# Low rank of a pair's two tiles turned together by one transpose

## Chip, cores and metric

The kernel runs on one core of one Trainium2 chip. The time is the device time of one execution in microseconds (us); the median of several runs counts.

## The reference

Two layers are computed on x, 32 samples of 64 rows by 1024 columns (2048 rows in all). The change touches the first one only. Its low rank part, cut to what matters:

```python
out = conv1d(x, weight, groups=4) + ctx + bias            # h, 2048 rows x 1024
y = h @ W.T + b                                           # 1024 x 1024
scores = h @ gate_w.T + gate_b                            # 4 ranks: 8, 16, 32, 64
pick the rank r with the highest softmax score (top 1; its weight is normalised to 1)
y = y + (h @ A[:r].T) @ B[:, :r].T                        # A: 64 x 1024, B: 1024 x 64
x = x + y
```

The second layer has the same form, with a mixture over 8 kernels in place of the convolution and a router over 8 experts of rank 16 in place of the ranks.

## The kernel before

**Tiles and pairs.** 128 rows are a tile, two tiles are a pair: tiles T = 0 to 15 and pairs g = 0 to 7 are the first layer, tiles 16 to 31 and pairs 8 to 15 the second. s = T % 2 says which tile of its pair a tile is. Pairs 0 and 1 are done plainly; from pair 2 (`FULL`) on the dense product of a pair is done in seven block products P1 to P7 in the manner of Strassen and Winograd. The code of each engine is one list written out by hand, with semaphores between the engines; the order in the code is the order on the engine.

**Two parts for each number.** The matmuls run in fp32r, and each float is split in a high part (ScalarE's cast, `a_hi`, `s_hi`, `ut_hi`) and the rest (VectorE's subtraction, `a_lo`, `s_lo`), so a product has three matmuls: high by high, high by low, low by high.

**A tile's low rank.** The plain matmuls (`plain`, L1265 and L1266, into `b_p`) also give the 64 low rank columns and the 4 scores of a tile. VectorE works out the gate (`gate0`, a chain of small instructions) and writes the gated low rank into `u_sb[:, s, :]`, 128 rows by 128, the 64 columns twice (L932). TensorE turns it by a transpose (`turn_u`, L1303) into `b_u`, so that the 64 ranks lie on partitions 0 to 63 and once more on 64 to 127. ScalarE casts all 128 partitions to `ut_hi` (L585) and the first 64 to `ut_lo` (L587); VectorE then overwrites partitions 64 to 127 of `ut_hi` with the rest (L890). `lb_hi` holds B twice, one above the other, so the one matmul `ut_hi` by `lb_hi` (L1311) gives high by high and low by high, and the second, `ut_lo` by `lb_lo` (L1313), the high by low part and the bias.

**A pair's order on TensorE** (g = 2 to 7): plain of both tiles, P1 into `b_x`, first half of the next pair's first convolution into `b_m` (L1231), **transpose of tile 2g**, P2 into `b_z`, second half of that convolution into `b_y`, **transpose of tile 2g + 1**, P4 into `b_w`, P5 into `b_y`, low rank of tile 2g into `b_z` and `b_p` (its first weight load waits for `utlo_done`, which L890 signals), a convolution, P6, a convolution into `b_z`, low rank of tile 2g + 1, P7, P3 and what is left.

**VectorE and ScalarE in that stretch.** VectorE: gates, `sum_mix` of the convolution's halves (L867), the `ut_hi` split of tile 2g between them, `a_lo` of the next pair's blocks A11 and A12 (L875, each after ScalarE's `a_hi`, L566), the `ut_hi` split of tile 2g + 1, and in pairs 3 to 6 four `prep_lo` splits (L824). In those four pairs GpSimd also forms sums of the second layer's weights (`praw`, L499 to L504) as soon as their load has landed; ScalarE casts them (L612).

## Time and profile before

| | |
|---|---|
| median of 3 runs | 506.79 us (505.94 to 506.85) |
| the profiled execution | 505.61 us |
| its span, first to last instruction | 503.9 us |
| TensorE's granted clock, mean | 1.000 of full |
| busy: TensorE, VectorE, ScalarE, GpSimd | 99%, 69%, 26%, 28% |
| first layer's pairs 2 to 7 | about 83 to 266 us of the span |

The busy shares count instructions in flight. Matmuls overlap, so a matmul's own duration is longer than what it adds to TensorE's list; the distance from one start, or from one piece of the chain, to the next is what it costs there.

### The profile page before, as it was taken

How to read it: one execution, taken by the hardware profiler on the slowest of the kernel's cores; microseconds unless marked ns; L12 is line 12 of the kernel's file. 1: busy time of each engine (PE TensorE's matmuls, PEld its weight loads, DVE VectorE, ACT ScalarE, POOL GpSimd, SP SyncE). 2: the span in 40 equal slices, each digit the busy share in tenths (PEclk: the TensorE clock that was granted, in tenths of full speed). 3: DMA queues.
4: the chain of work that ended last, by engine and by line, in shares of the span. 5: the costliest groups of instructions: out<-in, count | busy, mean ns of one | idle time of the engine just before them, and what ended most of it. 6: DMA issues, size and time to landing. Idle time of an engine off the chain costs nothing.

```text
span 503.9 us, 8309 instructions
## 1 busy us (share of the span) xinstructions
PE 499.1 (99%) x2981; PEld 467.7 (93%) x2981; DVE 347.9 (69%) x824; ACT 130.4 (26%) x272; POOL 142.0 (28%) x122
## 2 busy tenths in 40 slices
PE   8999999999999999999999999999999999999997
PEld 8999999999999999999999899999999999999986
DVE  3966988857766685776897975665747566574753
ACT  4732334212233122331252321210212111111200
POOL 1000010003443142431205462441516244152620
PEclk9999999999999999999999999999999999999999
DMA  8845204428476574657899752433425233340212
GB/s 317 320 144 166 91 1 148 157 89 262 163 245 195 196 231 171 197 184 268 273 410 339 298 168 87 145 102 126 130 69 161 85 129 103 134 138 19 103 47 84
DMA packets 41125, 84.34 MB, mean 167 GB/s; under 512 B 3803, under 2 KB 24667, under 8 KB 41084
## 3 DMA queue, kind: packets, MB, share of 16 engines
q1 hardware_dynamic: 31884, 61.16, 36.6%
q10 hardware_dynamic: 9200, 22.65, 12.3%
q8 instruction: 24, 0.39, 0.3%
q14 instruction: 17, 0.14, 0.1%
HBM read 58.82 MB, written 24.97 MB: 166 GB/s over the span
## 4 chain that ended last, share of the span: by engine, by line
PE 98%; DMA 1%; DVE 1%; issue 0%; ACT 0%; DVEq 0%
PE b_p L1265 10%; PE b_x L1283 7%; PE b_x L1286 7%; PE b_x L1285 7%; PE b_m L1231 6%; PE b_p L1266 5%; PE b_y L1285 5%; PE b_y L1286 5%; PE b_y L1283 5%; PE b_m L1241 3%; PE b_w L1283 2%; PE b_z L1285 2%; PE b_w L1285 2%; PE b_z L1286 2%; PE b_z L1283 2%; PE b_w L1286 2%
## 5 line engine op out<-in xcount | busy, mean ns | idle before, releaser
L566 ACT CAST a_hi<-mixed 128x512 fp32r<-128x512 f32 x63 | 38.1, 620 | 167.4 <-DVE mixed L870 88.3
L1265 PE MATMUL b_p<-wp,a_hi 128*128 128x464 f32 (+1 forms) x224 | 72.5, 377 | 0.0
L512 POOL TENSOR_TENSOR xs<-xs,mixw_sb 128x464 f32<-128x464 f32 (+1 forms) x28 | 36.3, 1307 | 115.2 <-DMA xs<-x_scratch 81.5
L1266 PE MATMUL b_p<-wp,a_lo 128*128 128x232 f32 (+1 forms) x224 | 60.0, 268 | 0.0
L882 DVE TENSOR_TENSOR s_lo<-mixed,s_hi 128x512 fp32r<-128x512 f32 x56 | 45.4, 834 | 20.5 <-ACT s_hi L578 20.5
L578 ACT CAST s_hi<-mixed 128x512 fp32r<-128x512 f32 x56 | 34.7, 621 | 77.3 <-POOL mixed L484 41.2
L875 DVE TENSOR_TENSOR a_lo<-mixed,a_hi 128x512 fp32r<-128x512 f32 x63 | 47.4, 779 | 9.4 <-ACT a_hi L566 8.8
L484 POOL TENSOR_TENSOR mixed<-mixed 128x512 f32<-128x512 f32 x13 | 17.6, 1353 | 120.9 <-DVE a_lo L875 120.9
L976 DVE TENSOR_TENSOR xs<-b_x,xs 128x464 f32<-128x464 f32 (+1 forms) x54 | 33.5, 620 | 22.9 <-PE b_x L1286 20.0
L1265 PEld LDWEIGHTS b_p<-wp,a_hi 128*128 128x128 f32 x224 | 42.0, 188 | 4.7
L1266 PEld LDWEIGHTS b_p<-wp,a_lo 128*128 128x128 f32 x224 | 42.7, 191 | 0.2
L1283 PE MATMUL b_y<-wb_hi,s_hi 128*128 128x464 f32 (+1 forms) x112 | 41.2, 368 | 0.0
L1285 PE MATMUL b_y<-wb_lo,s_hi 128*128 128x464 f32 (+1 forms) x112 | 41.1, 367 | 0.0
L1286 PE MATMUL b_y<-wb_hi,s_lo 128*128 128x464 f32 (+1 forms) x112 | 41.1, 367 | 0.0
L1231 PE MATMUL b_m<-first_in,blk 128*128 128x128 f32 x256 | 32.0, 278 | 0.2 <-DMA blk<-in_xblk 0.2
L976 DVE TENSOR_TENSOR xs<-b_y,xs 128x432 f32<-128x432 f32 (+1 forms) x28 | 17.4, 620 | 20.8 <-PE b_y L1286 20.0
L1231 PEld LDWEIGHTS b_m<-first_in,blk 128*128 128x128 f32 x256 | 30.8, 194 | 0.7 <-DMA blk<-in_xblk 0.5
L1283 PE MATMUL b_x<-wb_hi,s_hi 128*128 128x432 f32 (+1 forms) x80 | 30.5, 381 | 0.0
L1286 PE MATMUL b_x<-wb_hi,s_lo 128*128 128x432 f32 (+1 forms) x80 | 29.2, 365 | 0.0
L1285 PE MATMUL b_x<-wb_lo,s_hi 128*128 128x432 f32 (+1 forms) x80 | 29.2, 365 | 0.0
L1283 PEld LDWEIGHTS b_y<-wb_hi,s_hi 128*128 128x128 f32 x112 | 21.0, 188 | 2.0
L1286 PEld LDWEIGHTS b_y<-wb_hi,s_lo 128*128 128x128 f32 x112 | 21.0, 188 | 1.9
(260 smaller groups left out, 1210.0 us busy)
## 6 DMA issues: line engine op xcount, KB each, us to landing
blk<-x_scratch SPq DMA_DIRECT2D x16, 512.0 KB, 3.3
blk<-in_xblk SPq DMA_DIRECT2D x14, 516.0 KB, 3.9
xs<-in_x SPq DMA_DIRECT2D x16, 296.0 KB, 3.6
x_scratch<-xs SPq DMA_DIRECT2D x16, 296.0 KB, 4.5
w_raw<-in_wcat SPq DMA_DIRECT2D x8, 546.0 KB, 8.3
xs<-x_scratch SPq DMA_DIRECT2D x14, 280.0 KB, 3.2
out_dram<-xs SPq DMA_DIRECT2D x14, 280.0 KB, 2.5
praw<-in_wcat ACTq DMA_DIRECT2D x8, 464.0 KB, 6.1
```

What stands on the lines that cost most here:

```text
L512: pool.tensor_tensor(x_rows, x_rows, bbase[:, a:b], ALU.add).then_inc(x_biased[q], 1)
L566: act.copy(a_hi[:, op, :, :], mixed[:, op, :, :]).then_inc(ahi_done[op], 1)
L578: act.copy(s_hi[:, i, :, :], mixed[:, S_AT[i], :, :]).then_inc(shi_done[i], 1)
L875: dve.tensor_tensor(a_lo[:, op, :, :], mixed[:, op, :, :], hi(a_hi[:, op, :, :]), ALU.subtract).then_inc(alo_done[op], 1)
L882: dve.tensor_tensor(s_lo[:, i, :, :], mixed[:, S_AT[i], :, :], hi(s_hi[:, i, :, :]), ALU.subtract).then_inc(slo_done[i], 1)
L976: dve.tensor_tensor(x_rows, src[:, 0:HALF[l]], x_rows, ALU.add).then_inc(done, 1)
L1231: ins = pe.matmul(dst, blk[s][:, at + side:at + side + QB], taps, start=(side == 0), stop=(side == 1))
L1265: pe.matmul(both, x_hi, wp[:, k, :, 0:PLAIN[l]], start=(k == 0), stop=False, skip_group_check=True)
L1266: ins = pe.matmul(dst, x_lo, wp_hi[:, k, 0:PLAIN[l]], start=False, stop=(k == NCH - 1), skip_group_check=True)
L1283: pe.matmul(dst, x_hi[:, k, :], w_hi[:, k, :], start=(first and k == 0), stop=False, skip_group_check=not first)
L1285: pe.matmul(dst, x_hi[:, k, :], w_lo[:, k, :], start=False, stop=False, skip_group_check=not first)
L1286: ins = pe.matmul(dst, x_lo[:, k, :], w_hi[:, k, :], start=False, stop=(k == HK - 1), skip_group_check=not first)
```

## The change

In pairs 2 to 7 (`together`), the gate of tile 2g writes its 64 columns once into columns 0 to 63 of `u_sb[:, 0, :]`, that of tile 2g + 1 into columns 64 to 127. One transpose (`turn_pair`), at the place of the second, turns both: tile 2g lies on partitions 0 to 63 of `b_u`, tile 2g + 1 on 64 to 127. Each tile's high part is cast to its own half of `ut_hi[:, s, :]` and to `ut_lo[0:64]`, and VectorE writes the rest to the other half. The transpose of tile 2g goes, and its casts and its split move behind `split_a(A12, g + 1)` on both engines. Pairs 0, 1 and the second layer stay.

```diff
+        def together(T):
+            return 2 * FULL <= T < TILES
+        def turned_rows(s):
+            return slice(RANK * s, RANK * (s + 1))
...
@@ ScalarE, split_ut
+                if together(T):
+                    rows_ = turned_rows(s)
+                    act.copy(ut_hi[rows_, s, :], b_u[rows_, 0:P]).then_inc(uthi_done, 1)
+                    act.copy(ut_lo[0:RANK, s, :], b_u[rows_, 0:P]).then_inc(uthi_second, 1)
+                    return
...
@@ ScalarE, a pair
-                split_ut(2 * g)
+                if not together(2 * g):
+                    split_ut(2 * g)
                 if g < LAST:
                     split_a(A11, g + 1)
...
                 if g < LAST:
                     split_a(A12, g + 1)
+                if together(2 * g):
+                    split_ut(2 * g)
                 split_ut(2 * g + 1)
...
@@ VectorE, split_ut
+                if together(T):
+                    rows_ = turned_rows(s)
+                    dve.wait_ge(uthi_second, T + 1)
+                    dve.tensor_tensor(ut_hi[turned_rows(1 - s), s, :], b_u[rows_, 0:P], hi(ut_hi[rows_, s, :]),
+                                      ALU.subtract).then_inc(utlo_done, 1)
...
@@ VectorE, gate0
+                if together(T):
+                    dve.wait_ge(ut_done, T - s)
...
+                    if together(T):
+                        dve.tensor_scalar(u_sb[:, 0, RANK * s + r0:RANK * s + r], hid[:, r0:r],
+                                          kw[:, j:j + 1], None, ALU.mult).then_inc(gated, 1)
...
@@ VectorE, a pair
                 if g == FULL:
-                    split_ut(2 * g)
...
                 if g < LAST:
                     split_a(A11, g + 1)
                     split_a(A12, g + 1)
+                if together(2 * g):
+                    split_ut(2 * g)
                 split_ut(2 * g + 1)
...
@@ TensorE
+            def turn_pair(g):
+                pe.wait_ge(gated, 4 * (2 * g + 2))
+                pe.wait_ge(utlo_done, 2 * g)
+                pe.wait_ge(uthi_second, 2 * g)
+                pe.transpose(b_u[:, 0:P], u_sb[:, 0, :], ident[:, :]).then_inc(ut_done, 2)
...
-                turn_u(t1)
+                if not together(t1):
+                    turn_u(t1)
...
                     mixture(t1 + 2, 1, b_y)
-                    turn_u(t2)
+                    if together(t1):
+                        turn_pair(g)
+                    else:
+                        turn_u(t2)
```

On VectorE in pair 3, before the change, from the end of the second gate to the `prep_lo` splits (names are those above; `praw` are the weights in preparation):

```order
L932 TENSOR_SCALAR u_sb<-hid_sb,kw 128x2x32
L976 TENSOR_TENSOR xs<-b_x,xs 128x432 [waits x_loaded0,p1_done]
L867 TENSOR_TENSOR mixed<-b_m,ctx_row 128x8x64 [waits ctx_loaded,mix_done,slo_done3,slo_done1]
L890 TENSOR_TENSOR ut_hi<-b_u,ut_hi 64x128 [waits uthi_done]
L867 TENSOR_TENSOR mixed<-b_y,ctx_row 128x8x64 [waits ctx_loaded,mix_done,slo_done3,slo_done1]
L875 TENSOR_TENSOR a_lo<-mixed,a_hi 128x512 [waits ahi_done0]
L875 TENSOR_TENSOR a_lo<-mixed,a_hi 128x512 [waits ahi_done1]
L890 TENSOR_TENSOR ut_hi<-b_u,ut_hi 64x128 [waits uthi_done]
L824 TENSOR_TENSOR prep_lo<-praw,prep_hi 128x464 [waits prep_sum,phi_done] x4
```

The same stretch after the change (the line numbers are the changed kernel's):

```order
L956 TENSOR_SCALAR u_sb<-hid_sb,kw 128x32
L1003 TENSOR_TENSOR xs<-b_x,xs 128x432 [waits x_loaded0,p1_done]
L883 TENSOR_TENSOR mixed<-b_m,ctx_row 128x8x64 [waits ctx_loaded,mix_done,slo_done3,slo_done1]
L883 TENSOR_TENSOR mixed<-b_y,ctx_row 128x8x64 [waits ctx_loaded,mix_done,slo_done3,slo_done1]
L891 TENSOR_TENSOR a_lo<-mixed,a_hi 128x512 [waits ahi_done0]
L891 TENSOR_TENSOR a_lo<-mixed,a_hi 128x512 [waits ahi_done1]
L908 TENSOR_TENSOR ut_hi<-b_u,ut_hi 64x128 [waits uthi_second,uthi_done] x2
L840 TENSOR_TENSOR prep_lo<-praw,prep_hi 128x464 [waits prep_sum,phi_done] x4
```

The split of tile 6 stood ahead of the second `sum_mix`; now both splits stand behind both `a_lo`.

On TensorE in pair 3, before, around the transpose of tile 6 (the product after it is P2):

```order
L1231 MATMUL b_m<-first_in,blk 128x8x16 [waits blk_loaded0,sum_done,agg_read]
L1231 MATMUL b_m<-first_in,blk 128x8x16 x7
L1303 MATMUL b_u<-ident,u_sb 128x128 [waits uthi_second,utlo_done,gated]
L1283 MATMUL b_z<-wb_hi,a_hi 128x432 [waits sum_done]
L1285 MATMUL b_z<-wb_lo,a_hi 128x432
```

And after:

```order
L1257 MATMUL b_m<-first_in,blk 128x8x16 [waits blk_loaded0,sum_done,agg_read]
L1257 MATMUL b_m<-first_in,blk 128x8x16 x7
L1309 MATMUL b_z<-wb_hi,a_hi 128x432 [waits sum_done]
L1311 MATMUL b_z<-wb_lo,a_hi 128x432
```

The convolution is now followed by P2 directly; nothing else moves on TensorE up to the second transpose, which stays where it was.

## Rows read from the trace of the kernel before

**Rows 1.** The page: TensorE's busy time and share; then the chain that ended last.

```profile
PE 499.1 (99%) x2981; PEld 467.7 (93%) x2981; DVE 347.9 (69%) x824; ACT 130.4 (26%) x272; POOL 142.0 (28%) x122
...
PE 98%; DMA 1%; DVE 1%; issue 0%; ACT 0%; DVEq 0%
```

**Rows 2.** Times of TensorE's transposes, all 32 (ns, minimum, median, maximum).

```profile
L1303 PE MATMUL b_u<-ident,u_sb x32: 270/272/328, 33.8 to 487.1; 128*128 128x128 f32 x32
```

**Rows 3.** Chain of work, pair 4, around tile 8's transpose: start, duration, what.

```profile
154.81 0.56 PE b_m L1231 x5
155.37 0.11 PE b_u L1303
155.48 0.20 PE b_z L1283
```

**Rows 4.** Chain of work, pair 4, convolution straight ahead of a product.

```profile
166.27 0.56 PE b_m L1231 x5
166.83 0.20 PE b_x L1283
```

**Rows 5.** Order of time, pair 3, VectorE: start, duration, instruction, [idle before, releaser].

```profile
128.74 0.69 DVE L867 TENSOR_TENSOR mixed<-b_y,ctx_row 128x512 f32<-128x512 f32 x1 [2.25 <-PE b_y L1231]
130.11 3.13 DVE L875 TENSOR_TENSOR a_lo<-mixed,a_hi 128x512 fp32r<-128x512 f32 x2 [0.69 <-ACT a_hi L566]
133.28 0.29 DVE L890 TENSOR_TENSOR ut_hi<-b_u,ut_hi 64x128 fp32r<-64x128 f32 x1
```

**Rows 6.** Pair 3, VectorE, narrower stretch: the second a_lo by itself.

```profile
131.60 1.65 DVE L875 TENSOR_TENSOR a_lo<-mixed,a_hi 128x512 fp32r<-128x512 f32 x1
```

**Rows 7.** Pair 3, TensorE's weight loads at tile 6's first low rank matmul.

```profile
133.06 0.19 PEld L1311 LDWEIGHTS b_z<-lb,ut_hi 128*128 128x128 f32 x1
```

**Rows 8.** Pair 3, TensorE's matmuls at the same place.

```profile
133.45 0.36 PE L1313 MATMUL b_z<-lb,ut_lo 97*128 97x432 f32 x1
```

**Rows 9.** Pair 3, GpSimd.

```profile
127.47 1.19 POOL L499 TENSOR_TENSOR praw<-praw 128x464 f32<-128x464 f32 x1 [8.96 <-DMA praw<-in_wcat]
...
129.90 1.20 POOL L502 TENSOR_TENSOR praw<-praw 128x464 f32<-128x464 f32 x1
131.18 1.53 POOL L504 TENSOR_TENSOR praw<-praw 128x464 f32<-128x464 f32 x1
```

**Rows 10.** Tile 1's low rank, VectorE: end of the split that TensorE waited for.

```profile
47.13 0.29 DVE L890 TENSOR_TENSOR ut_hi<-b_u,ut_hi 64x128 fp32r<-64x128 f32 x1
```

**Rows 11.** Tile 1's low rank, weight loads.

```profile
47.48 0.19 PEld L1311 LDWEIGHTS b_z<-lb,ut_hi 128*128 128x128 f32 x1 [0.30 <-DVE ut_hi L890]
```

**Rows 12.** Tile 1's low rank, matmuls.

```profile
47.78 0.36 PE L1313 MATMUL b_z<-lb,ut_lo 97*128 97x432 f32 x1
```

**Rows 13.** VectorE, pairs 2, 4 and 7: the odd tile's ut_hi split.

```profile
100.09 0.29 DVE L890 TENSOR_TENSOR ut_hi<-b_u,ut_hi 64x128 fp32r<-64x128 f32 x1
...
163.33 0.29 DVE L890 TENSOR_TENSOR ut_hi<-b_u,ut_hi 64x128 fp32r<-64x128 f32 x1
...
253.20 0.29 DVE L890 TENSOR_TENSOR ut_hi<-b_u,ut_hi 64x128 fp32r<-64x128 f32 x1
```

**Rows 14.** Weight loads, the same pairs: the even tile's first low rank matmul.

```profile
101.16 0.19 PEld L1311 LDWEIGHTS b_z<-lb,ut_hi 128*128 128x128 f32 x1
...
164.07 0.19 PEld L1311 LDWEIGHTS b_z<-lb,ut_hi 128*128 128x128 f32 x1
...
255.30 0.19 PEld L1311 LDWEIGHTS b_z<-lb,ut_hi 128*128 128x128 f32 x1
```

**Rows 15.** Pair 3, VectorE, later: the last use of b_z.

```profile
136.46 0.60 DVE L976 TENSOR_TENSOR xs<-b_z,xs 128x432 f32<-128x432 f32 x1
```

**Rows 16.** Pair 3, weight loads: the convolution that overwrites b_z.

```profile
137.84 0.19 PEld L1231 LDWEIGHTS b_z<-first_in,blk 128*128 128x128 f32 x1
```

**Rows 17.** Pair 4, VectorE, ahead of that split.

```profile
161.12 1.20 DVE L875 TENSOR_TENSOR a_lo<-mixed,a_hi 128x512 fp32r<-128x512 f32 x1 [0.69 <-ACT a_hi L566]
162.61 0.69 DVE L875 TENSOR_TENSOR a_lo<-mixed,a_hi 128x512 fp32r<-128x512 f32 x1 [0.29 <-ACT a_hi L566]
```

More of the change, by code:

```diff
@@ L888, in split_ut @@
                 dve.wait_ge(uthi_done, T + 1)
-                if T < TILES:
+                if together(T):
[3 more added lines that the diff above has]
+                                      ALU.subtract).then_inc(utlo_done, 1)
+                elif T < TILES:
                     dve.tensor_tensor(ut_hi[RANK:P, s, :], src[RANK:P, :], hi(ut_hi[RANK:P, s, :]),
@@ L918, in gate0 @@
                 hid = hidden(T)
-                if T > 1:
+                if together(T):
+                    dve.wait_ge(ut_done, T - s)
+                elif T > 1:
                     dve.wait_ge(ut_done, T - 1)
@@ L931, in gate0 @@
                 for j, r in enumerate(RANKS):
-                    dve.tensor_scalar(u_sb[:, s, :].rearrange("p (d r) -> p d r", d=2)[:, :, r0:r],
-                                      hid[:, r0:r].unsqueeze(1).to_broadcast([P, 2, r - r0]),
-                                      kw[:, j:j + 1], None, ALU.mult).then_inc(gated, 1)
+                    if together(T):
+                        dve.tensor_scalar(u_sb[:, 0, RANK * s + r0:RANK * s + r], hid[:, r0:r],
+                                          kw[:, j:j + 1], None, ALU.mult).then_inc(gated, 1)
+                    else:
+                        dve.tensor_scalar(u_sb[:, s, :].rearrange("p (d r) -> p d r", d=2)[:, :, r0:r],
+                                          hid[:, r0:r].unsqueeze(1).to_broadcast([P, 2, r - r0]),
+                                          kw[:, j:j + 1], None, ALU.mult).then_inc(gated, 1)
                     r0 = r
@@ L1147, in _ @@
                     take_first(g)
-                if g == PAIRS - 1:
-                    split_ut(2 * g)
                 if g < LAST:
                     sum_mix(2 * g + 2, 0)
-                if g not in (FULL, PAIRS - 1):
+                if not together(2 * g):
                     split_ut(2 * g)
@@ L1515, in _ @@
                     mixture(t1 + 2, 1, b_y)
-                    turn_u(t2)
+                    if together(t1):
+                        turn_pair(g)
+                    else:
+                        turn_u(t2)
                 if g == FULL:
```

## The prediction, made before the changed kernel ran

> **What bounds the kernel now.** I read the page first. TensorE is busy 99% of the span and 98% of the chain that ended last is TensorE [rows 1]. So the end moves only by what TensorE's list gets shorter and by what TensorE newly waits for. Then the chain of work in order of time, around one of the transposes: it shows what each piece adds to the list, which a matmul's own duration does not. Then, in order of time, the stretch of each pair where the moved work has to be ready. The question for the reader is: how late does VectorE finish the split that tile 2g's low rank waits for, once that split stands behind both `a_lo`?
>
> **The removed transposes.** One goes in each of pairs 2 to 7, so six. A transpose lasts 0.27 us by its own duration [rows 2], but in the chain it is a piece of 0.11 us between the last of the convolution and P2 [rows 3]. Where a convolution is followed by a product with no transpose between, the next piece begins at once and the product's first piece is as long as there, 0.20 us [rows 3, 4]. So taking the transpose out leaves no gap of its own behind. 6 x 0.11 = 0.66 us less. The transpose overlaps its neighbours, and I take the 0.11.
>
> The Trainium skill (TensorE: Matmul & The Clock Gate, Part 4: PE-mode transpose) gives about 275 ns for a 128 by 128 transpose in a kernel's context. The duration here agrees (0.27 us), the piece of the chain does not. Six at that price would be 1.65 us, as in the second rival below.
>
> **Work on the other engines.** The four multiplications that end a gate write 64 columns rather than 128, the casts cover 64 partitions rather than 128 at the same free size, and the number of casts and splits is unchanged. The nearest row for the split, which now crosses to the other half of the partitions, is the one of before with the same 128 columns, 0.29 us [rows 5]. None of it is on TensorE's list; I cost it at nothing, covered by TensorE's products, except where it is late. What it costs without that cover is the next step.
>
> **The moved split, pair by pair.** Tile 2g's split now takes the place of tile 2g + 1's: directly behind the second `a_lo`. It then has to be done before the weight load of tile 2g's first low rank matmul, where the old one had been done long ago.
>
> Pair 2: the split at that place begins at 100.09 and ends at 100.38, the weight load begins at 101.16 [rows 13, 14]: 0.78 us to spare. Pair 4: 163.33 + 0.29 = 163.62 against 164.07, 0.45 us to spare; pairs 5 and 6 repeat pair 4 to within 0.01 us. Pair 7: 253.49 against 255.30, 1.8 us [rows 13, 14]. A signal takes about 0.06 us: tile 1's split ended at 47.13 + 0.29 = 47.42 and the load that waited for it began at 47.48 [rows 10, 11]. So these five pairs pass without a wait. That TensorE comes there 0.11 us earlier doesn't change it: the convolution half that starts the `sum_mix`, `a_hi`, `a_lo` chain also comes 0.11 us earlier.
>
> Pair 3 doesn't pass. There the two `a_lo` take 3.13 us together [rows 5], the second 1.65 us [rows 6], where the same instruction takes 0.69 us in pair 4 [rows 17]. In the same microseconds GpSimd works on `praw`, up to 131.18 + 1.53 = 132.71, and the second `a_lo` ends 0.54 us after that, at 133.25 [rows 6, 9]. In pair 4 the first `a_lo` is lengthened too, to 1.20 us, but it is over before the second is ready [rows 17]. GpSimd began so late in pair 3 because it waited for the load of `praw` [rows 9], 8.96 us. So the split there begins at 133.28 and ends at 133.57 [rows 5], and the weight load begins at 133.06 [rows 7]. After the change this load waits: it would begin at 133.57 + 0.06 = 133.63. A load that has waited has its second matmul 0.30 us later (47.48 to 47.78) [rows 11, 12], here at 133.93; before it was at 133.45 [rows 8], and with the transpose gone it would be at 133.34. The wait costs 133.93 - 133.34 = 0.59 us if GpSimd's end holds VectorE where it is, and 0.48 us if VectorE, too, comes 0.11 us earlier. I take 0.59, since what ends last ahead of the split is GpSimd, started by a load and not by TensorE.
>
> **What is queued behind.** Both splits behind each other put the four `prep_lo`, the taking of P5 and the first takings from `b_z` about 0.3 us later (one more split of 0.29 us). The closest user is the convolution that overwrites `b_z`: its last taking ends at 136.46 + 0.60 = 137.06, the weight load begins at 137.84 [rows 15, 16], 0.78 us to spare, more than 0.3. ScalarE's order only puts two casts behind two others; the `prep` casts have no user as near. Nothing more is added.
>
> **The sum.** -0.66 + 0.59 = -0.07 us, against the profiled execution's 505.61 us, which lies 1.18 us below the median of the runs shown. On the median: 506.79 - 0.07 = 506.7 us. This is no difference that can be measured: what can be told from no change here is about 0.2%, 1.0 us.
>
> **Rivals.**
>
> *No wait at all.* The wait in pair 3 hangs on when a load lands. If GpSimd's sums ended 0.6 us sooner or so, the second `a_lo` would end sooner by as much and the wait would be gone; landing later by about as much lets the first `a_lo` go ahead of a GpSimd sum and also shortens it. For it: GpSimd's start is set by a transfer [rows 9], which nothing ties to TensorE. Against: nothing in the change moves that load. Time: -0.66 us, 506.1 us; still within 0.2%.
>
> *The full duration comes back.* If each transpose gave back its 0.27 us [rows 2], six would give 1.63 us, and without a wait the time were 505.2 us, faster by 0.3%. Against: the chain's piece of 0.11 us [rows 3]. With the wait in pair 3 it were 505.8 us, at the edge.
>
> *Slower: the wait in all four preparing pairs.* If in pairs 4 to 6 as well the second `a_lo` is held by GpSimd. The point from which it decides: 0.45 - 0.06 = 0.39 us of lateness in a pair is free. With pair 3's 0.59 us in all four the sum is -0.66 + 2.36 = +1.7 us, 508.5 us; with three of the four it is +1.1 us, just slower. For it: the first `a_lo` of pair 4 is already lengthened to 1.20 us [rows 17]. Against: in those pairs it ends at 162.32, 0.29 us before the second is ready at 162.61 [rows 17], so GpSimd must be more than 0.6 us later for a first effect.
>
> The Trainium skill (SBUF — State Buffer, Who interferes with whom) says that a VectorE instruction with two inputs in SBUF and a GpSimd instruction that reads SBUF block each other whole, whichever came first holding. The second `a_lo` ending 0.54 us after GpSimd agrees. By that rule the split itself, with one input in PSUM, is not held, and only the order of the two engines at the moment decides pair 3.
>
> **How the numbers follow.** My forecast (a wait in pair 3 alone, 0.3 to 0.85 us): 0.56. No wait: 0.22. Full duration back: 0.09. Slower: 0.08. The remaining 0.05 is for what I don't see, half to each side. The predicted time is 506.7 us. Faster 0.11 (full duration, 0.02 of the rest), same 0.79, slower 0.10. The likeliest case with the runs' own spread of half a us to each side reaches from 506.0 to 507.3; the case without a wait pulls the low end to 505.5 (506.1 less that spread), and the high end stays at 507.3. Both far rivals lie outside.
>
> **What would show it.** In the chain of the changed kernel no `b_u` piece between the convolution into `b_m` and P2 in pairs 2 to 7, and P2 0.11 us closer to the convolution's end. Among the waits one of the weight load of `b_z<-lb,ut_hi` for VectorE's `ut_hi` split in pair 3, 0.5 to 0.6 us, none in pairs 2, 4, 5, 6 and 7. The first matmul of pair 8's plain part some 0.1 us earlier than now, with 0.2 to 0.7 us gained between single pairs. I am wrong if P2 comes by 0.2 us or more closer, if a `ut_hi` split lasts longer than 0.35 us, if weight loads wait in pairs 4 to 6, or if a wait arises at the overwriting of `b_z`.

## The result: 0.47% slower, where no difference was forecast

The changed kernel takes 508.52 us (median of 22 runs, 505.98 to 511.64), the kernel before 506.26 us (22 runs, 505.06 to 508.54) on the same chips. The ratio is 1.0047, interval [1.0033, 1.006]: slower by more than the 0.2% that a measurement here can tell, and above the range of 505.5 to 507.3. The profiled execution of the changed kernel took 507.78 us, its span is 506.0 us, 2.1 more than that of before, both at a granted clock of 1.0. In 8 of the 22 executions of the changed kernel TensorE's mean granted clock was 0.996 or 0.997 (beside the experiments, in 5 of 156 executions of the kernel before); the other 14 have a median of 508.2 us, so the clock is the smaller part of the loss (see e9).

The page of the changed kernel, the lines that answer to [rows 1]:

```profile
PE 499.3 (99%) x2975; PEld 467.3 (92%) x2975; DVE 346.5 (68%) x824; ACT 131.4 (26%) x272; POOL 141.8 (28%) x122
...
PE 84%; DMA 7%; DVE 3%; POOL 2%; issue 1%; ACT 1%; ACTq 0%; SPq 0%; DVEq 0%; POOLq 0%
```

TensorE has six matmuls fewer, and yet the end is no longer set by TensorE alone: 7% of the chain is DMA. The waits of TensorE in the changed kernel (engine, line, releaser: us in total, times, longest) name the two places:

```profile
PEld b_x L1309 <- DVE xs L1003: 1.8, 1, 1.8
PE b_x L1309 <- DVE xs L1003: 1.7, 1, 1.7
...
PEld b_z L1344 <- DVE ut_hi L908: 0.7, 1, 0.7
```

The last line is the forecast wait in pair 3. The first two are P7 of pair 7 (its weight load and its first matmul), and nothing in the prediction speaks of it.

**The removed transposes.** The chain of work of the changed kernel in pair 4, against [rows 3]:

```profile
154.15 1.78 PE b_m L1257 x16
155.94 0.20 PE b_z L1309
```

The convolution ends at 155.93, and P2 follows at once. Matching TensorE's matmuls of both traces one by one, the changed kernel's lead grows by 0.09 to 0.11 us at each of the six places, as the pieces of 0.11 us said. Ahead of pair 2, where the two kernels do the same, the changed one is already 0.18 us behind in this execution.

**Pair 3.** VectorE, the weight load and the matmuls of the changed kernel, against [rows 5, 7, 8], and GpSimd against [rows 9]:

```profile
130.12 3.25 DVE L891 TENSOR_TENSOR a_lo<-mixed,a_hi 128x512 fp32r<-128x512 f32 x2 [0.69 <-ACT a_hi L574]
133.39 0.61 DVE L908 TENSOR_TENSOR ut_hi<-b_u,ut_hi 64x128 fp32r<-64x128 f32 x2
```

```profile
133.73 0.19 PEld L1344 LDWEIGHTS b_z<-lb,ut_hi 128*128 128x128 f32 x1 [0.67 <-DVE ut_hi L908]
```

```profile
133.73 0.47 PE L1344 MATMUL b_z<-lb,ut_hi 128*128 128x432 f32 x1 [0.31 <-DVE ut_hi L908]
134.04 0.36 PE L1346 MATMUL b_z<-lb,ut_lo 97*128 97x432 f32 x1
```

```profile
131.29 1.52 POOL L512 TENSOR_TENSOR praw<-praw 128x464 f32<-128x464 f32 x1
```

GpSimd ends at 132.81, the second `a_lo` 0.56 us later at 133.37, the split for tile 6 at 133.69, and the load begins at 133.73. The second matmul is at 134.04 and was at 133.45. Before the wait the two traces were 0.01 us apart at this point, behind it 0.59: the wait costs 0.60 us, where the sum had 0.59.

**Pair 7.** The rest of the loss is here. The chain of work of the changed kernel at P7:

```profile
252.19 7.76 DMA xs<-in_x
...
259.97 0.34 DVE xs L1016
...
261.17 0.40 DVE wb_lo L844
...
262.20 0.61 DVE xs L1003
262.81 0.04 issue
262.86 0.47 PE b_x L1309
```

P7 writes `b_x` and has to wait until VectorE has taken P6 out of it. VectorE comes to that late, since two takings ahead of it waited for the rows of pair 7 to land, as VectorE's own rows say. First before, where the same two wait for nothing, then the changed kernel:

```profile
255.85 0.61 DVE L976 TENSOR_TENSOR xs<-b_y,xs 128x432 f32<-128x432 f32 x1
...
256.89 0.32 DVE L989 TENSOR_TENSOR xs<-b_p,xs 128x160 f32<-128x160 f32 x1
```

```profile
257.81 0.61 DVE L1003 TENSOR_TENSOR xs<-b_y,xs 128x432 f32<-128x432 f32 x1 [0.87 <-DMA xs<-in_x]
...
259.97 0.33 DVE L1016 TENSOR_TENSOR xs<-b_p,xs 128x160 f32<-128x160 f32 x1 [1.04 <-DMA xs<-in_x]
```

P7 comes at 262.86, before at 260.85:

```profile
260.85 0.39 PE L1283 MATMUL b_x<-wb_hi,s_hi 128*128 128x432 f32 x1
```

The shift against before grows there from +0.17 to +2.01 us, and to +2.2 us further on.

**Back to the root.** SP's queue on either side of that, first before, then the changed kernel:

```profile
237.37 0.32 SPq L342 DMA_DIRECT2D x_scratch<-xs  x1
242.91 0.33 SPq L337 DMA_DIRECT2D xs<-in_x  x1
243.34 0.85 SPq L342 DMA_DIRECT2D x_scratch<-xs  x2
247.91 0.83 SPq L337 DMA_DIRECT2D xs<-in_x  x2
```

```profile
238.31 0.32 SPq L350 DMA_DIRECT2D x_scratch<-xs  x1
244.07 0.33 SPq L345 DMA_DIRECT2D xs<-in_x  x1
244.50 0.85 SPq L350 DMA_DIRECT2D x_scratch<-xs  x2
251.81 0.81 SPq L345 DMA_DIRECT2D xs<-in_x  x2
```

A pair's rows are stored and loaded in quarters (0 and 1 are the halves of the first tile's rows, 2 and 3 of the second's). The first line is the store of quarter 2 of pair 6. SP then waits until it has landed and loads that quarter for pair 7 (`stored(2, g)`, `load_x(2, g + 1)`). Only behind that stand the stores of quarters 3 and 1, and behind their landing the loads of these two. The store of quarter 2 is 0.94 us later. The two others are 1.16 us later, and their landing, which the next loads wait for, takes 7.3 us where it took 4.6 (243.34 to 247.91, 244.50 to 251.81). Only the second of the two lands later: 6.8 us after its own issue, before 4.1 us; the first takes 3.1 us and took 3.2. What runs beside them is a load of 928 KB on ScalarE's queue, in the changed kernel at:

```profile
244.56 0.65 ACTq L743 DMA_DIRECT2D wp_place<-in_wcat  x1
```

Before, it was issued 0.95 us behind the first of the two stores (244.29), now 0.06 us behind it.

The lateness of quarter 2's store comes from the split that was moved, by way of a transfer. VectorE in pair 6, before and then the changed kernel:

```profile
225.34 0.29 DVE L890 TENSOR_TENSOR ut_hi<-b_u,ut_hi 64x128 fp32r<-64x128 f32 x1
225.67 2.30 DVE L824 TENSOR_TENSOR prep_lo<-praw,prep_hi 128x464 fp32r<-128x464 f32 x4
```

```profile
225.97 0.66 DVE L908 TENSOR_TENSOR ut_hi<-b_u,ut_hi 64x128 fp32r<-64x128 f32 x2
226.67 1.75 DVE L840 TENSOR_TENSOR prep_lo<-praw,prep_hi 128x464 fp32r<-128x464 f32 x3
```

`prep_lo` begins 1.00 us later: 0.27 because TensorE is behind by that much (0.18 from the start of the trace, and what pair 3's wait leaves beyond the transposes gone by then), 0.37 for the second split, and 0.36 more because the second `sum_mix` of the pair comes late (see the open points). ScalarE stores `prep_lo`, waits for the landing, loads it home, and only then makes `a_hi`. ScalarE before and in the changed kernel:

```profile
234.88 1.14 ACT L566 CAST a_hi<-mixed 128x512 fp32r<-128x512 f32 x2 [9.02 <-DMA ts_lo_scratch<-prep_lo]
```

```profile
235.82 1.15 ACT L574 CAST a_hi<-mixed 128x512 fp32r<-128x512 f32 x2 [8.61 <-DMA ts_lo_scratch<-prep_lo]
```

The lateness passes through the wait for this transfer nearly whole, 0.94 us. VectorE's `a_lo` follows, and behind it on VectorE's list the taking that releases quarter 2's store.

A second part is the landing of that store: 5.5 us before, 5.7 in the changed kernel, and 5.4 to 6.6 us over all profiled executions. Counted from the start of pair 7, e1 and e13 issue it only 0.10 us later than before, it lands after 6.6 and 6.5 us, and the two stores behind it come at +5.5 and +5.4. So in some executions most of their lateness comes from this landing and not from the split. What makes it longer wasn't tried.

### The profile page after: what moved, and what is told of

It reads as the page before. It is cut to its first block, busy times and chain, and to the rows that moved or that the text cites. A ratio compares the mean times of both kernels' runs of the same rounds, so it can differ in the third digit from the quotient of the medians.

```text
span 506.0 us, 8309 instructions
## 1 busy us (share of the span) xinstructions
PE 499.3 (99%) x2975; PEld 467.3 (92%) x2975; DVE 346.5 (68%) x824; ACT 131.4 (26%) x272; POOL 141.8 (28%) x122
## 4 chain that ended last, share of the span: by engine, by line
PE 84%; DMA 7%; DVE 3%; POOL 2%; issue 1%; ACT 1%; ACTq 0%; SPq 0%; DVEq 0%; POOLq 0%
PE b_p L1291 8%; PE b_x L1309 6%; PE b_x L1312 6%; PE b_x L1311 6%; PE b_m L1257 4%; PE b_p L1292 4%; PE b_y L1311 4%; PE b_y L1309 4%; PE b_y L1312 4%; PE b_m L1267 3%; DMA x_scratch<-xs 2%; PE b_z L1311 2%; PE b_w L1309 2%; PE b_w L1311 2%; PE b_z L1309 2%; PE b_z L1312 2%
```

## The experiments

In the table every time is counted from the start of pair 7 (its first matmul `b_p<-wp,a_hi`, in the changed kernel at 239.27), in each kernel's profiled execution: when the stores of quarters 3 and 1 were issued, when the loads behind them were, how long lies between, when VectorE took `b_p` (which needs the second of these loads), and what P7's first matmul waited. The executions differ by chance already ahead of pair 2, by up to 0.8 us, so spans of single executions are not compared without that. The load of `wp_place` was issued at +5.29 to +5.34, but at +6.75 and +6.33 in e7 and e12.

| kernel | median us | ratio to before | stores | loads | between | `b_p` taken | P7 waits |
|---|---|---|---|---|---|---|---|
| before | 506.26 | | +4.35 | +8.92 | 4.6 | +17.89 | 0 |
| changed | 508.52 | 1.0047 | +5.22 | +12.54 | 7.3 | +20.70 | 1.7 |
| e9, changed again | 509.14 | 1.0060 | +5.75 | +13.72 | 8.0 | +22.30 | 2.9 |
| e1, not pair 3 | 507.07 | 1.0014 | +5.53 | +12.15 | 6.6 | +20.38 | 1.3 |
| e3, splits early | 505.48 | 0.9984 | +5.06 | +9.81 | 4.8 | +18.07 | 0 |
| e5, not pair 6 | 504.82 | 0.9971 | +4.38 | +9.15 | 4.8 | +18.24 | 0 |
| e7, load later | 505.69 | 0.9987 | +5.88 | +10.52 | 4.6 | +19.77 | 1.3 |
| e8, before + lateness | 509.11 | 1.0032 | +5.82 | +12.85 | 7.0 | +19.87 | 0.3 |
| e12, e3 + e7 | 505.20 | 0.9979 | +4.97 | +9.49 | 4.5 | +18.06 | 0 |
| e13, pair 6 alone | 506.24 | 0.9997 | +5.40 | +12.16 | 6.8 | +19.41 | 0.2 |
| e14, pair 3 alone | 506.32 | 0.9995 | +5.10 | +12.43 | 7.3 | +19.35 | 0.1 |
| e15, not pair 7 | 505.94 | 0.9986 | +5.69 | +12.67 | 7.0 | +19.36 | 0 |
| e16, pair 7 alone | 505.80 | 0.9990 | +4.41 | +8.96 | 4.6 | +18.25 | 0 |
| e17, stores first | 505.20 | 0.9983 | +2.25 | +6.91 | 4.7 | +18.53 | 0 |
| e18, before, stores first | 506.05 | 1.0001 | +2.42 | +6.84 | 4.4 | +18.54 | 0 |

Four more runs (e2, e6, e10, e11) have a fault in their edits, and e4 touches none of this; they are not in the table. In a pair that is taken back, tile 2g's split stood in its general place on VectorE's list, behind the first `sum_mix`. But in the kernel before, pairs 2 and 7 have it further ahead: ahead of the splits of S, and ahead of that `sum_mix`. So in e2, e6 and e10 (pair 7), and in e10 and e11 (pair 2), the second tile's transpose came 0.5 to 1.3 us later for waiting for a split, which neither kernel does in the trace. They are told, but settle nothing about a pair; e13 to e16 are the same questions without that fault.

**e1: all but pair 3.**

```
 def together(T):
-    return 2 * FULL <= T < TILES
+    return 2 * FULL <= T < TILES and T // 2 != 3
```

> The change, but pair 3 is left as before. Two places theory (the wait for VectorE's split in pair 3 costs 0.6 us by itself; some 1.8 us more arise in pair 7, where the rows of pair 7 are loaded late): about 0.5 us less than the changed kernel if the late loads stay, so 1.7 to 2.0 us above the kernel before; in the trace no wait of the weight load of b_z in pair 3, and a wait of the first matmul of P7 in pair 7. Rival, one place theory (the late split in pair 3 pushes everything behind it, the late loads too): all of the loss goes, at or 0.6 us under the kernel before.

507.07 us, ratio 1.0014 [0.9985, 1.0043]. The wait in pair 3 is gone from the trace, that of P7 in pair 7 is still there (1.3 us). Three of its twelve executions had a granted clock of 0.996 or 0.997, and they are the three slowest (509.4 to 510.8 us). So pair 3 is a part of the loss at most, and pair 7's wait doesn't need it.

**e2: all but pairs 6 and 7.**

```
-    return 2 * FULL <= T < TILES
+    return 2 * FULL <= T < 12
```

> The change in pairs 2 to 5 only, pairs 6 and 7 as before. Two places theory: the loss in pair 7 goes, the wait in pair 3 stays: 4 x 0.11 = 0.44 us saved, 0.6 us lost, within 0.3 us of the kernel before; the loads of pair 7's rows are issued near 248 us, not 252 us. Rival (the lateness that reaches pair 7 comes from pair 3 on): still 1.5 us or more above the kernel before.

506.18 us, 0.9999 [0.9973, 1.0025]. P7 doesn't wait, but the second transpose of pair 7 does, 1.3 us, by the fault named above.

**e3: both splits early,** on ScalarE and VectorE ahead of the next pair's `a_hi` and `a_lo`.

```
-                if not together(2 * g):
-                    split_ut(2 * g)
+                split_ut(2 * g)
+                if together(2 * g):
+                    split_ut(2 * g + 1)
                 if g < LAST:
                     split_a(A11, g + 1)
...
-                if together(2 * g):
-                    split_ut(2 * g)
-                split_ut(2 * g + 1)
+                if not together(2 * g):
+                    split_ut(2 * g + 1)
```

> The change, with both ut splits of a pair moved ahead of a_hi and a_lo of block A11, on ScalarE and on VectorE, directly behind the second sum_mix, where VectorE idles 0.69 us until ScalarE has cast. If late splits are the only cause of both losses (two places theory with its root in the order of VectorE), no weight load waits in pair 3, prep_lo and all behind it comes at the time of before or earlier, the loads of pair 7 are issued near 248 us, and the time is 0.66 us under the kernel before (0.4 to 1.0). Rival (lateness has another root, such as the one transpose itself or chance in the transfers): about as slow as the changed kernel, 1.5 us or more above before.

505.48 us, 0.9984 [0.9961, 1.0007]; span 503.1, 0.8 less than before. There is no wait in pair 3 and none in pair 7, and TensorE ends 0.73 us ahead of before. Some 0.33 of that stood already ahead of pair 2, by chance; each removed transpose but the last then gave 0.09 to 0.10 us, the last 0.05, and 0.1 us is lost again behind them.

**e4: what a transpose costs in TensorE's list.** The kernel before with four more transposes beside each of 12, 48 in all, written where nobody reads.

```
+                if 2 * FULL <= T < TILES:
+                    for _ in range(4):
+                        pe.transpose(b_u[:, 2 * P:3 * P], u_sb[:, s, :], ident[:, :])
                 pe.transpose(b_u[:, P * s:P * s + P], u_sb[:, s, :], ident[:, :]).then_inc(ut_done, 1)
```

> The kernel before with four more transposes of the same u_sb in front of each of the twelve transposes of tiles 4 to 15, into unused columns of b_u: 48 more, output unchanged. If a transpose costs the 0.11 us of its piece in the chain: 5.3 us slower (up to 6 with knock-on in transfers). If it costs its 0.27 us: 13 us slower.

510.91 us, 1.0089 [1.0059, 1.012], 4.8 us over the median of before on that chip. The chain of work of e4 in pair 4:

```profile
155.30 1.78 PE b_m L1231 x16
157.08 0.43 PE b_u L1305 x4
157.52 0.11 PE b_u L1306
157.63 0.20 PE b_z L1283
```

Four more are 0.43 us, and TensorE is 5.1 us later at the end: 0.11 us each. The price of 0.27 us, 13 us for 48, is refuted.

**e5: all but pair 6.**

```
-    return 2 * FULL <= T < TILES
+    return 2 * FULL <= T < TILES and T // 2 != 6
```

> The change in all pairs but pair 6, which is as before. If the loss in pair 7 has its root in pair 6, where the four prep_lo come one split later, it goes: 5 x 0.11 = 0.55 us saved, 0.6 us lost in pair 3, so within 0.3 us of the kernel before. If its root is the moved order within pair 7, or chance: 1.2 us or more above before.

504.82 us, 0.9971 [0.9954, 0.9988], the lowest median of the study. Against the changed kernel one pair has been taken back, and 3.7 us of the median have gone. The gain over before is more than its five transposes explain (0.55 us, 0.11%), though the interval reaches to 0.12%.

**e6: all but pair 7,** as e5 with `T < 14`.

> The change in all pairs but pair 7. If the root of the loss is pair 6: the rows of pair 7 are loaded late here too, and the loss stays, 1 to 2 us above before. If it is pair 7's own moved order: 5 x 0.11 = 0.55 us saved, 0.6 us lost in pair 3, within 0.3 us of before.

507.61 us, 1.0023 [1.0003, 1.0042], with the fault; the wait of 1.2 us is at the second transpose of pair 7. See e15.

**e7: the load of `wp_place` later.** In the changed kernel four small copies stand ahead of its issue on ScalarE.

```
                     act.wait_ge(pl_done, 2 * PAIRS)
+                    for i in range(4):
+                        act.copy(spare[:, P * i:P * (i + 1)], ones[:, :]).then_inc(first_hi, 1)
+                    act.wait_ge(first_hi, 5)
```

> The change, with four small copies on ScalarE, which idles there, in front of the 928 KB load of the second layer's plain weights in pair 7, so that the load is issued some 0.8 us later. If the two stores of pair 6's rows, issued 0.07 us ahead of it in the changed kernel and 0.94 us ahead before, are late because they share the transfer engines with this load: stores have landed within 5 us instead of 7.3, the first matmul of P7 in pair 7 waits less than 0.5 us instead of 1.7, and the time is 1 to 1.8 us under the changed kernel, 0.3 to 1 us above before. If the collision is not the cause: as slow as the changed kernel.

505.69 us, 0.9987 [0.9972, 1.0003]: 2.8 us under the median of the changed kernel, with the change itself whole. The stores, 0.87 us ahead of the load now, land after 4.6 us. In the profiled execution (507.31 us, over the median) P7 waits 1.3 us nonetheless, but not for the rows: no taking waits for them. VectorE waits for ScalarE's casts of the held back load and of the next one, and the takings stand behind:

```profile
255.72 2.16 DVE L854 TENSOR_TENSOR wp<-wp_place,wp 128x928 fp32r<-128x928 f32 x2 [1.73 <-ACT wp L671]
260.70 1.12 DVE L848 TENSOR_TENSOR wb_lo<-wb_raw,wb_hi 128x928 fp32r<-128x928 f32 x1 [0.47 <-ACT wb_hi L666]
```

So this cure has a price of its own, and its median shows the sum of both.

**e8: the lateness alone.** The kernel before, with four small subtractions on VectorE in pair 6 ahead of `prep_lo`.

```
+                if g == PREP_LAST:
+                    for i in range(4):
+                        dve.tensor_tensor(spare[:, P * i:P * (i + 1)], ident[:, :], ones[:, :], ALU.subtract)
                 if PREP_FIRST <= g <= PREP_LAST:
                     for b in (0, 1, 3, 2):
```

> The kernel before, with four small subtractions (128 by 128, into unused memory, 0.6 to 1 us in all) on VectorE in pair 6 alone, between the odd tile's ut split and the prep_lo; no transpose is touched. If lateness of VectorE in pair 6 is what starts the loss in pair 7: pair 6's stores are issued within 0.3 us of the load of the plain weights, the rows of pair 7 are loaded late, and the kernel is 1 to 2 us slower than before. If VectorE's lateness there is harmless: no change, within 0.3 us of before.

509.11 us (505.95 to 510.64), 1.0032 [1.0009, 1.0056]. Nothing of the change is in this kernel, and its median is as high as that of the changed one. Its executions fall in two groups: five at 506.0 to 507.5 us, as before, and seven at 508.8 to 510.6, of which five had a granted clock of 0.995 to 0.997. So the lateness makes the loss in a part of the executions. The profiled one (507.46 us) is of the lower group: the stores are at +5.82, 7.0 us lie between, the second transpose of pair 7 waits 0.3 us and P7 another 0.3. It was 0.77 us behind before already ahead of pair 2, and loses 0.9 us in pair 7.

**e9: the changed kernel again,** on another chip.

> The changed kernel once more, for a second profiled execution. Two things are asked of it. The wait in pair 3 should come only if GpSimd starts its sums about 12.7 to 12.8 us after the pair's first plain matmul (before and the first trace of the changed kernel); from 13.0 us on the two a_lo take about 0.8 us each and nothing waits. The late rows in pair 7 should come again, with the wait of P7 or of the transpose's successor: time 1.7 to 3 us above before.

509.14 us, 1.006 [1.0038, 1.0081]. Both waits are there again, 0.7 us for the weight load in pair 3 and 2.9 us at P7. Here the wait has a sequel. In stretches of the profile (busy us and instructions of each engine, then PEclk, TensorE's granted clock as a share of full speed) during the wait, behind it, and later:

```profile
261.30:264.20 2.90, 0.00 (x0) 0.00 (x0) 2.82 (x6) 0.62 (x1) 0.00 (x0) 1.00 1.02 419
264.90:268.10 3.20, 3.20 (x10) 2.92 (x10) 3.01 (x6) 0.62 (x1) 0.00 (x0) 0.50 1.01 421
269.00:275.00 6.00, 6.00 (x36) 5.63 (x36) 4.17 (x7) 1.24 (x2) 4.38 (x3) 1.00 0.95 299
```

TensorE did nothing for 2.9 us; its granted clock then fell from 1.00 to 0.50, 1.2 GHz in place of 2.4, for at least the 3.2 us shown. P7's matmuls start 0.36 us apart there and 0.20 at full clock, which puts TensorE 1.6 us further back. In the changed kernel's profiled execution, with 1.7 us of waiting, the clock stays at 1.00. The executions at 0.993 to 0.997 (8 of 22 of the changed kernel, 5 of 12 of e8, 4 of 9 of e9) fit such a fall, but only this one was profiled.

**e10 and e11: pair 3 alone, pair 7 alone** (`together` true for that pair).

> The change in pair 3 alone. If its wait were there in every execution, 0.59 - 0.11 = 0.5 us slower than before; as five of seven profiled executions with pair 3 in the new order or near it had no wait there, I expect -0.1 to +0.5 us, a median within 0.3 us of before. If pair 3's lateness by one split reaches pair 7's loads through the transfers, more than 1 us slower.

> The change in pair 7 alone. In the kernel before, the transpose of tile 15 follows tile 14's split on VectorE by less than 0.1 us in the profiled execution, so any lateness of VectorE there stops TensorE (as in the trace of the kernel that left pairs 6 and 7). With pair 7 changed that link is gone. If this link costs the kernel before something in most executions, the median falls by 0.5 us or more, more than the 0.11 us of one transpose; if not, it falls by 0.1 us, which can't be told from nothing.

507.02 us, 1.0013 [1.0001, 1.0026], and 507.04 us, 1.001 [0.9995, 1.0024]. Both have the fault: 0.9 us in pair 2 in both, 0.5 us in pair 7 in e10. The link to the trace of e2 in the second expectation was to this same fault. In e11 the stores came at +5.21, 0.13 us ahead of the load, 7.2 us lay between, and P7 waited 0.5 us, though pair 6 is as before. Both are inconclusive; e14 and e16 are the clean ones.

**e12: e3 and e7 together.**

> Both cures together: the early splits in all pairs and the load of the plain weights held back on ScalarE. If the stores of pair 6 and this load collide in part of the executions of the early kernel too, the median falls below its 505.5 us, to 504.5 to 505.0 us, 1.2 to 1.8 us under before, with no wait in pairs 3, 6 or 7; if not, it stays at 0.6 us under before.

505.2 us, 0.9979 [0.9962, 0.9997]: not told apart from e3.

**e13 to e16: single pairs, each split in the place that before has for it.**

```
 e13:  return T < TILES and T // 2 == 6
 e14:  return T < TILES and T // 2 == 3
 e15:  return 2 * FULL <= T < 14
 e16:  return T < TILES and T // 2 == 7
+                apart = not together(2 * g)
                 if g == FULL:
+                    if apart:
+                        split_ut(2 * g)
                     for i in S_ORDER:
                         split_s(i, g)
                 if g != PAIRS:
                     take_first(g)
+                if g == PAIRS - 1 and apart:
+                    split_ut(2 * g)
                 if g < LAST:
                     sum_mix(2 * g + 2, 0)
-                if not together(2 * g):
+                if g not in (FULL, PAIRS - 1) and apart:
                     split_ut(2 * g)
```

> The change in pair 6 alone; every other pair is as before, VectorE's place of each split included (the kernels that took single pairs back so far had one split of tile 2g moved behind a sum_mix or behind the splits of S, and the second transpose waited for it). Theory (pair 6 is the root of the loss): prep_lo in pair 6 comes 0.6 us or more late, the stores of pair 6's rows too (relative to pair 7's start at +5.0 or later where before had +4.35), the rows of pair 7 land after +12 where before had +8.92, and P7 in pair 7 waits 1 us or more; 0.11 us come back from the one transpose, so the profiled span is 0.5 to 2 us longer and the ratio 1.002 or more. Rival (lateness has to add up over pairs 2 to 6, or pair 3 carries the loss): rows in pair 7 at +9 to +10, no wait, ratio between 0.999 and 1.001.

506.24 us, 0.9997 [0.9979, 1.0015]. The stores are late, 6.8 us lie between, and the loads of the rows go out at +12.16, as expected. But P7 waits 0.2 us where 1 us or more was expected, and the median shows no loss: pair 6 alone is not enough, and my number was wrong.

> The change in pair 3 alone, all other pairs as before, order of the splits included. Theory (pair 6 is the root; pair 3 costs 0.59 us in those executions in which GpSimd is ahead of the first a_lo, nothing in others): span +0.5 us or -0.1 us, no wait in pair 7, ratio 1.000 to 1.001. Rival (pair 3's wait is what makes the changed kernel slow): ratio 1.002 or more, the wait of the weight load of b_z for the split present and the rows of pair 7 late.

506.32 us, 0.9995 [0.9976, 1.0015]. There is no wait for the split in pair 3 in this execution. Pair 6 is untouched here and the rows are late all the same (+12.43), since quarter 2's store took 6.1 us to land and not 5.5. So the kernel before is itself close to this edge.

> The change in pairs 2 to 6, pair 7 as before with its split at the old place. Theory (lateness is made in pair 6 and only shows in pair 7): the rows of pair 7 still land after +11, the wait of 1 us or more is there, in P7 or in what comes for x_scratch's rows next, and the ratio is 1.002 to 1.006. Rival (the later split in pair 7 itself holds VectorE's takings up and makes the wait): no wait in pair 7, ratio 0.998 to 1.000.

505.94 us, 0.9986 [0.9972, 1.0001], where my theory had a loss. The rows are as late as in the changed kernel, stores first, then loads, SP in e15:

```profile
244.04 1.00 SPq L350 DMA_DIRECT2D x_scratch<-xs  x2
251.01 0.81 SPq L345 DMA_DIRECT2D xs<-in_x  x2
```

and yet VectorE's takings wait less, and P7 doesn't at all (a part of it is hidden, for the second transpose of pair 7 had waited 0.2 us for VectorE):

```profile
255.84 0.61 DVE L1003 TENSOR_TENSOR xs<-b_y,xs 128x432 f32<-128x432 f32 x1 [0.21 <-DMA xs<-in_x]
...
257.71 0.33 DVE L1016 TENSOR_TENSOR xs<-b_p,xs 128x160 f32<-128x160 f32 x1 [0.74 <-DMA xs<-in_x]
```

Issued at the same time in the pair, the second row load is there for VectorE 6.3 us after its issue in e15 (251.39 to 257.71), in the changed kernel after 7.8.

> The change in pair 7 alone, pairs 2 to 6 as before. Theory (pair 6 is the root): rows of pair 7 at +8.9 to +9.2 as before, no wait in pair 7, one transpose less, ratio 0.999 to 1.0005. Rival (pair 7's own split order makes the wait): P7 waits 1 us or more, ratio 1.002 or more.

505.8 us, 0.999 [0.9975, 1.0005]. The rows are at +8.96 and nothing waits, as expected. Pair 7 alone isn't enough either.

So neither pair 3, 6 nor 7 carries the loss alone (pairs 2, 4 and 5 weren't tried alone), and rows that are late don't always cost: in the table P7 waits 0.2 us at most where `b_p` is taken by +19.4, 0.3 in e8 (+19.87), and 1.3 to 2.9 us where it is taken at +20.4 or later; e7, which waits for something else, stands apart. Whether the late rows are the cause at all had to be tried with the change left whole. The last two runs do that.

**e17: the stores first.** In the changed kernel SP issues the stores of quarters 3 and 1 of pair 6 as soon as their rows are taken, ahead of the wait for quarter 2. **e18** is the same move in the kernel before.

```
                     store_x(3, g - 1)
                     sp.wait_ge(fin12, g)
                     store_x(1, g - 1)
+                    if g == PAIRS - 1:
+                        stored(2, g - 1)
+                        load_x(2, g)
...
                 store_x(2, g)
-                stored(2, g)
-                if g < LAST and not turns:
-                    load_x(2, g + 1)
+                if g != PAIRS - 2:
+                    stored(2, g)
+                    if g < LAST and not turns:
+                        load_x(2, g + 1)
```

> The changed kernel with one thing moved on SP's queue between pairs 6 and 7: the stores of pair 6's second rows (quarters 3 and 1) go out as soon as VectorE has taken them, ahead of the wait for the landing of quarter 2's store and of that quarter's load, behind which they stood. Their rows are taken 2.9 us after pair 7's start, and they were issued at +5.2. Theory (the loss is made where these stores meet the 928 KB load of wp_place, issued at +5.29, and the rows of pair 7 land late for it): stores at +2.5 to +3.5, loads of the rows issued by +9, no wait of P7 in pair 7, span 503.0 to 503.9 us (six transposes gone, with or without pair 3's wait), ratio 0.997 to 0.999. Rival (pair 7's later split or other queues hold P7, not the stores): P7 still waits 1 us or more in pair 7, ratio 1.002 or more.

> The kernel before with the same move on SP's queue alone. Theory (the kernel before has its stores at +4.35, 0.94 us ahead of the load of wp_place, and loses nothing there in most executions): ratio 0.999 to 1.000, the profile without a wait in pair 7, as before. Rival (the kernel before, too, loses time there in many executions): ratio 0.998 or less, and the changed kernel with the same move is then no more than 0.13% faster than this one.

e17: 505.2 us (504.56 to 506.38), 0.9983 [0.9972, 0.9993]. e18: 506.05 us, 1.0001 [0.9991, 1.0012]. SP in e17, the three stores and then the three loads:

```profile
238.09 4.27 SPq L350 DMA_DIRECT2D x_scratch<-xs  x3
244.60 2.46 SPq L345 DMA_DIRECT2D xs<-in_x  x3
```

The stores are 3 us ahead of the load of `wp_place`, the loads go out at +6.91, and VectorE takes without waiting:

```profile
256.76 0.61 DVE L1007 TENSOR_TENSOR xs<-b_y,xs 128x432 f32<-128x432 f32 x1
...
257.80 0.32 DVE L1020 TENSOR_TENSOR xs<-b_p,xs 128x160 f32<-128x160 f32 x1
```

Of TensorE's waits only one is left, the one at the start of the kernel that before has too:

```profile
PE b_y L1376 <- POOL ones L471: 1.1, 1, 1.1
```

The one transpose for two, the later split and pair 7's order are all in e17. In its profiled execution TensorE is 0.73 us behind before ahead of pair 2, by chance, and 0.07 at the end: 0.66 us come back, six times 0.11. With the stores ahead of the large load the change makes the kernel 0.17% faster (0.66 of 506 us is 0.13%), with the order as it was 0.47% slower. The kernel before gains nothing by the move; in its profiled execution the second transpose of pair 7 waits 0.4 us, where the expectation had no wait, and P7 doesn't. That the loss hangs on where these stores, and the loads behind them, are issued is shown. That it is the meeting with the load of `wp_place` which delays their landing rests on the times in the table and on e7's median.

## Why the prediction was wrong

**The removed transposes: right.** 0.11 us each, at all six places and in e4; 0.66 us in all. The rival with the whole duration is refuted: 0.27 us is how long one lasts, 0.11 is what it adds.

**Pairs 2, 4, 5, 6 and 7 without a wait for the split: right.** TensorE waits for `ut_hi` in none of them.

**The wait in pair 3: right in size, not in how often.** 0.60 us against 0.59, with the second `a_lo` ending 0.56 us after GpSimd. But it is there in some executions alone. Counted from pair 3's first `b_p<-wp,a_hi` matmul (0.2 us less than by the count in the expectation of e9), GpSimd's sums began at 12.46 to 12.63 in five profiled executions (before 12.50, changed 12.52, e9 12.54, e3, e12), and there each `a_lo` took 1.4 to 1.7 us; in 13 others they began at 12.80 or later and neither took more than 1.12 us. Two don't fit this line: e14, at 12.62, has short ones, and e4, at 12.88, has 1.46 and 1.59 us (its `a_lo` come 0.44 us later for the added transposes). Ten profiled kernels have the late split in pair 3, and TensorE waits for it by 0.6 us in two, the changed kernel and e9, and by under 0.1 us in e15. The prediction's rival without a wait named this very condition, with 0.6 us of shift needed, and gave it 0.22; 0.2 to 0.3 us were enough. e14, pair 3 alone, costs nothing that can be told.

**"Nothing more is added": this step failed.** It put the four `prep_lo` and the takings behind them about 0.3 us late and looked for their nearest user among TensorE's matmuls (`b_z`, 0.78 us to spare). `b_z` is indeed not waited for. But `prep_lo` has another reader, a transfer: ScalarE stores it, waits until it has landed and loads it home before the next `a_hi`. Lateness on VectorE went through that wait nearly whole (1.00 us to 0.94), through `a_lo`, quarter 2's store and its landing, into two more stores that had 0.94 us to the 928 KB load. I had also said that the `prep` casts have no user as near. The lateness was 1.0 us and not 0.3 (0.6 when counted from the start of pair 6, and 0.3 as forecast in e1 and e13), and e8 shows that lateness at this place alone makes the loss in a part of the executions (median 509.11 us). The step had no term either for what the clock takes after a wait (1.6 us in e9) or for a landing that varies by 1 us. In the changed kernel the path costs 1.84 us at P7, in the median 2.3 us with everything.

**The likeliest sum.** -0.66 + 0.59 had both terms right in the profiled execution; the term left out was +1.84 us at P7, and 0.2 us behind it. With the 0.18 us from ahead of pair 2 these are the 2.2 us by which TensorE ends later. Without the term left out (e17) the kernel is at 0.9983 [0.9972, 0.9993], which holds the -0.66 us (-0.13%) of the prediction's rival without a wait.

**The slower rival** gave 508.5 us, and 508.52 was measured, but by another mechanism: the wait in all four preparing pairs didn't come. That number was right by chance.

**What stays open.** Why the changed kernel loses and e13 and e15 don't, with rows loaded equally late, isn't settled. In the traces the row loads are issued 0.18 us (changed), 0.32 (e1) and 1.57 us (e9) behind the second 928 KB load of `wb_raw`, and `b_p` is taken at +20.4 to +22.3; in e13, e14 and e15 they are issued from 0.19 us ahead of it to 0.03 behind, and `b_p` is taken at +19.4. e8 (0.06 us behind, `b_p` at +19.9) and e11 (0.03 behind, +19.5) fit in between; e7, where P7 waits for other loads, says nothing on it. This is an ordering of eight executions and was not tried by itself. Open too is what makes quarter 2's store land after 5.4 us in one execution and 6.6 in another. Also open is why the second `sum_mix` of pair 6 comes 0.36 us late; it does so in the changed kernel, e3, e6, e7, e9, e12, e15 and e17, and not in e5, nor in e1 and e13, whose pair 6 is changed too.

## What to carry to other kernels

When an instruction is put into an engine's list, follow every instruction behind it to all of its readers, the DMA queues among them: a store that is waited for can carry lateness on nearly undiminished, and may set it down far away, here some 35 us later. A queue that waits for one transfer ahead of issuing two others that are ready is worth looking at before anything else; moving this wait made the same change a gain. And price a removed instruction by its piece of the chain, not by its duration, then ask of each slack that is left (here 0.94 us between stores and a large load) whether the change eats it.

## What the runs showed of the hardware

Two stores of 296 KB each on one queue, issued 0.4 to 0.5 us apart, had both landed by 4.4 to 4.8 us after the first was issued (counted to the issue of the load that waits for them) where that was 0.6 to 3 us ahead of a 928 KB load on another queue, and 6.6 to 8.0 us after it where it was from 0.2 us ahead to 0.5 us behind. In between, e3 (0.26 us ahead) has 4.8 us and e2 (0.41 us) 5.9.

A 128 by 128 fp32 transpose among other matmuls adds 0.11 us to TensorE's list (48 of them 5.1 us), while its own duration is 0.27 us.

The same VectorE `a_lo` takes 0.69 us alone and up to 1.68 us beside GpSimd's sums. In pair 3 the two together take 2.9 to 3.4 us where GpSimd starts at 12.63 or before, and 1.5 to 2.1 us from 12.80 on, with e14 and e4 as exceptions.

After 2.9 us in which TensorE did nothing (e9), its granted clock was 0.50 for at least 3.2 us, which cost 1.6 us; after 1.7 us (the changed kernel) it stayed at 1.00.
